# Decoder layer with expert routing on one core: row numbers inside the residual rows, normalised rows scattered as fp16 halves and turned by the loading DMA, two PSUM banks for z

## The chip, the cores and the metric

One core of one Trainium2 chip runs the whole program in one launch. The metric is the time of one execution on the device in microseconds, the median of several runs.

## The reference

The input is x, 4 batches of 512 rows of 512 floats. Three sub-layers follow one another, each with a layer norm (eps 1e-5) in front and a residual sum behind:

```python
x = x + attn(layernorm(x))     # 16 heads of 32, elu features, no softmax
x = x + experts(layernorm(x))  # one of 4 experts for each token, by token id
x = x + ffn(layernorm(x))      # ternary weights, 512 -> 2048 -> 512
# attn:    q = k = elu(x Wqk + bqk), v = silu(x Wv + bv), u = silu(x Wu + bu)
#          out = q (k^T v) within each head; (u * layernorm(out)) Wo + bo
# experts: e = min(clip(id) // 6250, 3); y = (silu(x W[e]^T) * (x W[e]^T)) W[e]^T
# ffn:     (silu(x up^T) * (x gate^T)) down^T, each weight rounded to -1, 0, 1 times its mean magnitude
```

All three weights of the expert layer are the same tensor `ctx`, 4 x 512 x 512. A product there is one matrix z, used as silu(z) * z.

## The kernel before, in words

Rows are handled in 16 tiles of 128 rows (`NT` = 16, four of a batch, `T` = 4; `K` = 4 chunks of 128 columns). Products are made of fp16 halves (a high part and the rest) in three passes of a 128x512 product for each chunk, so one full product is 12 matmuls. `resid` holds all 2048 rows of the residual in SBUF, fp32. Five engines run programs of their own, in fixed order, and meet at semaphores. SP issues all plain loads and the turning ones, in one order and on one queue. POOL issues the indirect scatters and computes the 1/sqrt of each layer norm (`rsqrt`, L307).

**Attention.** The loop over batches runs on every engine (`batch` on POOL L333, ACT L478, DVE L825, PE L1156), pipelined: in batch b the products q, v, k, u of b are mixed with the output projection (`project`, L1121) and the second layer norm of b - 1 (`second_norm`, L802), and with the weights of the later stages (`ctx_part`, `magnitudes`). At its end PE forms k^T v and q (k^T v); ACT copies the four results from PSUM (`o_copies`, L538), sums the magnitudes of a 1 MB piece of weights (`magnitudes`, L471), and starts the next batch with the exponentials of q (L483). DVE takes statistics of the copies (`head_stats`), and before the next batch waits until the scatters of b - 1 have landed, since `n2` is used again.

**Sorting by expert.** The rows are sorted by expert through DRAM. `routing_positions` gives each row its place `pos`. `scatter` (L320) sends a tile of normalised rows, fp32, out of `n2` to `sorted_tokens`. `scatter_residual` (L325) sends a tile of residual rows to `sorted_residual`, and `scatter_ids` (L329) one 4-byte row number of each row to `sorted_ids`. The scatters of batches 0 and 1 are issued in the batches behind them. For batch 2 the normalised rows go early in batch 3 and the residual rows after the last head normalisation. At the end of batch 3 POOL handles one tile after the other: `rsqrt_tile` of tile t, then `scatter` of tile t - 1 (L399 to L406); then a memset that DVE waits for before it makes the next signs, the four residual scatters, and all 16 scatters of row numbers. DVE's part of this is `last_sum` (residual sum, statistics) and `last_norm` (L921 to L962).

**Experts.** `STEPS` = 19 steps; each takes 128 sorted rows (one tile) with one expert, and a tile that has rows of several experts is done several times (`own` masks). SP loads sorted tile i into one of three slots of `n2` (`sorted_tile`, L232); PE transposes it into the bank `tx_ps` (`xs_transpose`, L1306), ACT copies the high half to `x3T` (`xs_hi`, L585) and DVE subtracts for the low half (`xs_lo`, L965). In step i (`expert_step`, L1329) PE does: z of step i (`first`), the transposes of tile i + 1, the second product of step i - 1 (`second`), in steps 0 to 9 the turning of one unit of ternary weights for the last layer (`unit_transposes`, L1265), and the transposes of h. DVE adds the result to the sorted residual (`y_add`, L970), which SP loads a batch at a time (`sorted_residual`, L235). SP's order here (L242 to L267):

```python
sp.wait_ge(s["scattered"], 16 * NT)
for i in range(3): sorted_tile(i)
unit(1, 0)                       # after sign_b >= 1
sp.wait_ge(s["x1_sent"], 16 * NT)
sorted_residual(0)
unit(1, 1); unit(1, 2)           # after sign_b >= 2, 3
for n in range(6):
    sp.wait_ge(s["tx_mm"], n + 1)
    sorted_tile(n + 3)
    if n % 2 == 0: sorted_residual(1 + n // 2)
    unit(2 + n // 3, n % 3)      # after sign_b >= n + 4
```

A unit is 1 MB of weights. `signs_of` (L904) on DVE makes two signed bf16 planes of it. PE fills its wait for the last rows with 100 small matmuls (`keep_busy`, L1303).

**Last layer.** The third layer norm writes halves to `x3h`, and SP turns them with `dma_start_transpose` from SBUF into `x3T` (`x3_turned`, L269). The outputs are scattered to their rows with `row_id`, which SP loads from `sorted_ids`.

Of the kernel before, what the change touches and what calls it, by code (L numbers as in the profile page):

```python
# [31 lines left out]
P = 128  # L32
# [17 lines left out]
def decoder(nc, x, itok, ctx_w, Wqk, bqk, Wv, bv, Wu, bu, Wo, bo, ln_g, ln_b, W_up, W_gate, W_down, out):  # L50
# [5 lines left out]
    def sem(name):  # L56
# [16 lines left out]
    xs_v = xs_dram.rearrange("(c p) d -> p c d", p=P)  # L73
    x1_v = x1_dram.rearrange("(c p) d -> p c d", p=P)
    id_v = id_dram.rearrange("(c p) o -> p (c o)", p=P)


    resid = sb("resid", [P, NT, D])
# [32 lines left out]
    tok_id = sb("tok_id", [P, NT], I32)  # L111
    row_id = sb("row_id", [P, NT], I32)
# [8 lines left out]

    xT = late[:, 0].bitcast(F16).rearrange("p (i k s) -> p i k s", i=2, k=K)
# [18 lines left out]
    xs_slot = [n2[:, i] for i in range(3)]  # L141
# [11 lines left out]
    z_ps, y_ps, tx_ps, th_ps, q_ps = ps[0], ps[1], ps[2], ps[3], ps[4:8]  # L153
# [4 lines left out]
        att_in3 stage_in0 stage_in1 scattered x1_sent id_sent id_in x1_in0 x1_in1 x1_in2 x1_in3 xs_in0 xs_in1 xs_in2 unit_in0 unit_in1 unit_in2  # L158
# [6 lines left out]
        x2_stat x2_aggr x2_norm tk_mm k_copy u_mm u_act kv_mm kv_evac o_mm o_copy o_stat o_aggr o_norm  # L165
        tx_mm xs_hi xs_lo z_mm z_act h_mul th_mm h_hi h_lo y_mm y_evac sign_a sign_b unit_mm unit_copy
# [17 lines left out]
    def _(sp):  # L184
# [47 lines left out]
        def sorted_tile(i):  # L232
            sp.dma_start(xs_slot[i % 3], xs_v[:, i]).then_inc(s[f"xs_in{i % 3}"], 16)

        def sorted_residual(b):  # L235
            sp.dma_start(resid[:, T * b:T * b + T], x1_v[:, T * b:T * b + T]).then_inc(s[f"x1_in{b}"], 16)
# [18 lines left out]
        for n in range(6):  # L255
            sp.wait_ge(s["tx_mm"], n + 1)
            sorted_tile(n + 3)
            if n % 2 == 0:
                sorted_residual(1 + n // 2)
            sp.wait_ge(s["sign_b"], n + 4)  # L260
            unit(2 + n // 3, n % 3)
        for i in range(9, NT):
            sp.wait_ge(s["tx_mm"], i - 2)
            sorted_tile(i)

        sp.wait_ge(s["id_sent"], 16 * NT)
        sp.dma_start(row_id[:, :], id_v, allow_slow_non_contiguous=True).then_inc(s["id_in"], 16)  # L267
# [8 lines left out]
        for b in range(B):  # L276
            x3_turned(b)


    @block.gpsimd  # L280
    def _(pool):
# [10 lines left out]
        def late_constants():  # L292
# [12 lines left out]
            pool.iota(tok_id[:, :], pattern=[[P, NT]], base=0, channel_multiplier=1).then_inc(s["starts_made"], 1)  # L305
# [23 lines left out]
        def scatter_ids(b):  # L329
            for n in range(T * b, T * b + T):  # L330
                pool.indirect_dma_start(id_dram, row_of(n), tok_id[:, n:n + 1], None).then_inc(s["id_sent"], 16)

        def batch(b):  # L333
# [75 lines left out]
        for b in range(B):  # L409
            scatter_ids(b)  # L410
# [4 lines left out]
        def send_out(b):  # L415
            for t in range(T):
                pool.wait_ge(s["out_made"], T * b + t + 1)
                pool.indirect_dma_start(out_rows, bass.IndirectOffsetOnAxis(ap=row_id[:, T * b + t:T * b + t + 1], axis=0),  # L418
# [4 lines left out]
        pool.wait_ge(s["id_in"], 16)  # L423
# [7 lines left out]
        for t in range(T):  # L431
            pool.wait_ge(s[f"out_done{t}"], 16 * B)
# [3 lines left out]
    def _(act):  # L436
# [25 lines left out]
        def gated_hi(b, k):  # L462

            act.wait_ge(s["a_mul"], K * b + k + 1)
# [13 lines left out]
        def batch(b, first, last):  # L478
# [50 lines left out]
            if first:  # L529
                magnitudes(b, 1)  # L530
            o_copies(b)
# [28 lines left out]
        with act.Fori(1, B - 1) as b:  # L560
# [5 lines left out]
        o_copies(B - 1)  # L566
        magnitudes(B - 1, 1)
# [6 lines left out]
        gated_hi(B - 1, 0)  # L574
# [5 lines left out]
        gated_hi(B - 1, 3)  # L580
        unit_copies(0, 0)
        unit_copies(0, 1)


        def xs_hi(i):  # L585
            act.wait_ge(s["tx_mm"], i + 1)
            act.activation(x3T[:, i // T, 0, :, (i % T) * P:(i % T + 1) * P], tx_ps.rearrange("p (k s) -> p k s", k=K),
                           ACT.Copy).then_inc(s["xs_hi"], 1)
# [7 lines left out]
        def expert_step(i):  # L596
            act.wait_ge(s["z_mm"], i + 1)
            act.wait_ge(s["h_mul"], i)
            act.activation(sil, z_ps[:, :], ACT.Silu, scale=1.0 / CTX_SCALE).then_inc(s["z_act"], 1)
            if i + 1 < NT:  # L600
                xs_hi(i + 1)
# [10 lines left out]
        xs_hi(0)  # L612
# [33 lines left out]
    def _(dve):  # L646
# [155 lines left out]
        def second_norm(b, t):  # L802
            normalise(2, n2[:, t], x_tile(T * b + t), t, "x2_norm")
# [21 lines left out]
        def batch(b, first, last):  # L825
# [60 lines left out]
            if first:  # L886
                routing_positions()
            if last:
# [12 lines left out]
            if not first:  # L901
                dve.wait_ge(s["scattered"], 16 * T * b)
# [537 lines left out]
```

## Time and profile before

| | us |
|---|---|
| median of 3 runs | 774.2 |
| lowest and highest | 771.91, 776.83 |
| the profiled execution | 772.51 |
| its span | 770.8 |

The span is the time from the first to the last instruction of the profiled execution; its own time is 1.7 us more. Busy over the span: PE 93%, PE's weight loads (PEld, beside PE) 49%, DVE 49%, ACT 35%, POOL 19%. The mean granted clock of PE is 0.979 of full speed. In the rows, `L1082` is a line of kernel.py, which for products and transposes is the line of a helper; x12 is a count; what stands in brackets is the idle time of the engine ahead of the instruction and what ended it.

### The profile page before, as it was taken

The page shows a single profiled execution, that of the slowest core. Times are in us where ns is not written, and L with a number is a line of the kernel's source. Part 1 is how long each engine was busy: PE and PEld are TensorE (multiplying, and loading weights), DVE is VectorE, ACT ScalarE, POOL GpSimd, SP SyncE. Part 2 cuts the span into 40 slices and gives each one's busy share as a digit, 9 for nine tenths or more (in the row PEclk, how much of TensorE's full clock was granted, in tenths as well). Part 3 has the DMA queues.
Part 4 walks back from the last instruction along what each step waited for, and adds up shares of the span by engine and source line. Part 5 has one row for each costly group of instructions (what it writes and reads, how often), then busy time and mean ns, then how long its engine had stood idle before and what let it go on. Part 6 is the DMA issues. An engine that isn't in the chain of part 4 may idle for free.

```text
span 770.8 us, 11599 instructions
## 1 busy us (share of the span) xinstructions
PE 713.1 (93%) x3979; PEld 379.5 (49%) x4008; DVE 378.3 (49%) x622; ACT 273.2 (35%) x426; POOL 146.5 (19%) x202
## 2 busy tenths in 40 slices
PE   7999999999998852999999999999999999999994
PEld 5465466466464721656554444444444444444441
DVE  5566776776767522566455333353333433342232
ACT  4366455455463420444323222222222223222220
POOL 4204532332344860000000000020000200020001
PEclk9999999999999985999999999999999999999998
DMA  8823045044055579761102000011001200010001
GB/s 244 330 102 118 1 135 193 0 147 181 1 182 200 206 102 179 261 225 42 29 1 49 8 14 14 14 44 38 14 14 14 68 14 14 14 54 1 0 1 54
DMA packets 48182, 64.00 MB, mean 83 GB/s; under 512 B 25360, under 2 KB 25360, under 8 KB 47120
## 3 DMA queue, kind: packets, MB, share of 16 engines
q1 hardware_dynamic: 43792, 50.89, 23.2%
q0 software_dynamic: 4352, 12.60, 4.2%
q8 instruction: 25, 0.41, 0.3%
q14 instruction: 13, 0.11, 0.0%
HBM read 46.69 MB, written 12.59 MB: 77 GB/s over the span
## 4 chain that ended last, share of the span: by engine, by line
PE 76%; DVE 7%; DMA 7%; issue 3%; ACT 3%; SPq 2%; POOL 1%; DVEq 0%; ACTq 0%; POOLq 0%
PE bank L1352 28%; PE bank L1082 25%; PE bank L1362 13%; PE bank L1075 4%; DMA n<-sorted_tokens 3%; DVE region L773 2%; PE bank L1239 2%; PE bank L1275 2%; PE bank L1253 2%; DMA stage<-in_L_ffn_W_up_dram 2%; DVE late L769 1%; SPq L229 1%; DMA w_att<-nrm 1%; DMA stage<-in_L_attn_Wv_dram 1%; PE bank L1413 1%
## 5 line engine op out<-in xcount | busy, mean ns | idle before, releaser
L1352 PE MATMUL bank<-w_att,region 128*128 128x512 f16 (+1 forms) x1024 | 231.2, 379 | 2.6 <-DMA w_att<-nrm 2.6
L1352 PEld LDWEIGHTS bank<-w_att,region 128*128 (+1 forms) x1024 | 100.1, 98 | 123.7 <-issue 3.3
L1045 DVE SCALAR_TENSOR_TENSOR tmp<-tmp,hk,bank 128x512 f32<-128x512 f32 x64 | 47.8, 747 | 155.9 <-PE bank L1352 155.4
L1362 PE MATMUL bank<-region,tmpA 128*128 (+1 forms) x452 | 111.3, 379 | 1.5
L310 POOL TENSOR_SCALAR ve<-mv 128x1 f32<-128x1 f32 (+1 forms) x37 | 9.2, 248 | 452.9 <-DVE mv L983 338.4
L1082 PE MATMUL bank<-late,w_att 128*128 128x512 f16 x384 | 86.5, 381 | 1.9 <-DVE region L816 1.9
L621 ACT ACTIVATE tmp<-bank,qs 128x512 f32<-128x512 f32 x64 | 44.0, 687 | 116.6 <-PE bank L1352 116.6
L628 ACT ACTIVATE tmpA<-tmp 128x512 f16<-128x512 f32 x62 | 39.0, 629 | 120.2 <-DVE tmp L1045 120.2
L1362 PEld LDWEIGHTS bank<-region,tmpA 128*128 128x128 f16 x480 | 46.8, 98 | 56.8 <-DVE stage L1029 0.9
L1049 DVE TENSOR_TENSOR tmpA<-tmp,tmpA 128x512 f16<-128x512 f32 x62 | 42.9, 693 | 44.1 <-ACT tmpA L628 44.1
L1082 PEld LDWEIGHTS bank<-late,w_att 128*128 128x128 f16 x384 | 37.4, 98 | 44.5 <-DVE region L816 2.8
L1082 PE MATMUL bank<-w_moe,w_att 128*128 x228 | 52.4, 380 | 4.6 <-issue 2.9
L1082 PE MATMUL bank<-w_moe,tmpA 128*128 x228 | 53.7, 386 | 0.0
L1082 PE MATMUL bank<-w_att,region 128*128 128x512 f16 x192 | 42.4, 379 | 4.0 <-DVE region L777 2.0
L1082 PE MATMUL bank<-w_att,late 128*128 128x512 f16 x192 | 42.8, 379 | 0.0
L552 ACT ACTIVATE region<-bank 128x512 bf16<-128x512 f32 x48 | 24.8, 605 | 40.6 <-PE bank L1275 40.6
L418 POOL DMA_INDIRECT out_dram<-stage,row_id x16 | 16.2, 1011 | 108.7 <-DVE stage L1029 106.9
L1082 PEld LDWEIGHTS bank<-w_moe,w_att 128*128 x228 | 22.2, 97 | 29.1 <-issue 7.5
L1082 PEld LDWEIGHTS bank<-w_moe,tmpA 128*128 128x128 f16 x228 | 22.6, 100 | 24.9 <-issue 2.3
L977 DVE SCALAR_TENSOR_TENSOR resid<-bank,own,resid 128x512 f32 x19 | 14.3, 750 | 37.6 <-PE bank L1082 23.6
L1075 PE MATMUL bank<-ident,n 128*128 128x128 f32 x64 | 10.1, 283 | 23.3 <-DMA n<-sorted_tokens 23.3
L1082 PEld LDWEIGHTS bank<-w_att,region 128*128 128x128 f16 x192 | 18.3, 98 | 26.9 <-issue 2.7
(145 smaller groups left out, 847.5 us busy)
## 6 DMA issues: line engine op xcount, KB each, us to landing
stage<-in_L_ffn_W_up_dram SPq DMA_DIRECT2D x8, 1024.0 KB, 5.9
stage<-in_L_ffn_W_gate_dram SPq DMA_DIRECT2D x8, 1024.0 KB, 5.4
stage<-in_ctx_dram SPq DMA_DIRECT2D x4, 1024.0 KB, 6.6
stage<-in_L_ffn_W_down_dram SPq DMA_DIRECT2D x4, 1024.0 KB, 7.3
nrm<-in_L_ffn_W_down_dram SPq DMA_DIRECT2D x4, 1024.0 KB, 7.5
n<-sorted_tokens SPq DMA_DIRECT2D x16, 256.0 KB, 5.4
resid<-sorted_residual SPq DMA_DIRECT2D x4, 1024.0 KB, 15.4
resid<-in_x_dram SPq DMA_DIRECT2D x1, 3072.0 KB, 19.1
```

Of the source, the lines that this page charges most:

```text
L418: pool.indirect_dma_start(out_rows, bass.IndirectOffsetOnAxis(ap=row_id[:, T * b + t:T * b + t + 1], axis=0), out_slot[t], None).then_inc( ...
L552: act.activation(dst, src, ACT.Copy).then_inc(s["unit_copy"], 1)
L621: act.activation(sil, up_ps[:, :], ACT.Silu, scale=qs[:, 0:1]).then_inc(s["up_act"], 1)
L628: act.activation(dst[:, cc % 2, 0], h32, ACT.Copy).then_inc(s["hid_hi"], 1)
L773: dve.tensor_tensor(aT[:, 1, k], a32[:, k % 2], aT[:, 0, k], ALU.subtract).then_inc(s["a_lo"], 1)
L1045: dve.scalar_tensor_tensor(out=h32, in0=sil, scalar=hk[:, 0:1], in1=gate_ps[:, :], op0=ALU.mult, op1=ALU.mult).then_inc(s["hid_mul"], 1)
L1049: dve.tensor_tensor(dst[:, cc % 2, 1], h32, dst[:, cc % 2, 0], ALU.subtract).then_inc(s["hid_lo"], 1)
L1075: mm = pe.transpose(dst[:, i * P:(i + 1) * P], src(i), ident[:, :])
L1082: mm = pe.matmul(dst, lhs(*step), rhs(*step), start=(start and n == 0), stop=(stop and n == len(steps) - 1))
L1239: mm = pe.matmul(kv_ps[:, cut], kk[:, t, cut], vv[:, t, cut], start=(t == 0), stop=(t == T - 1))
L1352: mm = pe.matmul(dst, w[:, bass.ds(cf_c, 1), k * P:(k + 1) * P].rearrange("p a n -> p (a n)"), x3T[:, bass.ds(b, 1), i, k].rearrange("p a ...
L1362: mm = pe.matmul(ffy_ps[t][:, :], hid[:, parity, i, t * P:(t + 1) * P], tern[2][:, bass.ds(c, 1)].rearrange("p a n -> p (a n)"), start=(st ...
```

## The change

- `resid` becomes the first 512 words of rows of 513 (`rows`). The 513th holds the row number, made by the iota that filled `tok_id`. `sorted_residual` has rows of 513 words (2052 bytes), scatters and loads move them whole, and `row_id` is a view of the 513th words. `scatter_ids`, `sorted_ids`, and the load of `row_id` are gone.
- The second layer norm writes fp32 rows to `region[:, 5]` (the place of aT), for the last batch to `region[:, 1]`. ACT copies them to fp16 high halves (`n2_hi`), DVE subtracts for the low halves (`n2_lo`), both in `n2h`, which is `n2` seen as fp16. `scatter` waits for `n2_lo` and sends 2 x 512 halves of each row, as many bytes as before.
- In the experts' stage `sorted_tile` is a `dma_start_transpose` from DRAM straight to its place in `x3T`. `xs_transpose`, `xs_hi` and `xs_lo` are gone; SP goes by `z_mm` in place of `tx_mm`, PE's `first` waits for the tile's own transfer.
- z has two PSUM banks (the old one and the one of the tile transposes).
- Orders: POOL's `rs_o` comes ahead of the scatters in each batch; those of batch 2 move behind the last head normalisation's rsqrt. ACT's batches 1 and 2 are written out instead of looped. `n2_hi` stands ahead of `o_copies` in batches 1 and 2, `n2_lo` ahead of `head_stats`. DVE's wait for landed scatters at a batch's end goes. SP instead of POOL waits for the last output scatters.

```diff
-    xs_dram = nc.dram_tensor("sorted_tokens", (NT * P, D), F32, kind="Internal").ap()
-    x1_dram = nc.dram_tensor("sorted_residual", (NT * P, D), F32, kind="Internal").ap()
-    id_dram = nc.dram_tensor("sorted_ids", (NT * P, 1), I32, kind="Internal").ap()
+    xs_dram = nc.dram_tensor("sorted_halves", (NT * P, 2 * D), F16, kind="Internal").ap()
+    x1_dram = nc.dram_tensor("sorted_residual", (NT * P, D + 1), F32, kind="Internal").ap()
-    resid = sb("resid", [P, NT, D])
+    rows = sb("rows", [P, NT, D + 1])
+    resid = rows[:, :, 0:D]
+    row_id = rows[:, :, :].bitcast(I32)[:, :, D:D + 1]
+    n2h = n2[:].rearrange("p t d -> p (t d)").bitcast(F16).rearrange("p (t h d) -> p t h d", t=T, h=2)
+    second_rows = lambda b: region[:, 1] if isinstance(b, int) and b == B - 1 else region[:, 5]
...
         def sorted_tile(i):
-            sp.dma_start(xs_slot[i % 3], xs_v[:, i]).then_inc(s[f"xs_in{i % 3}"], 16)
+            sp.dma_start_transpose(
+                out=x3T[:, i // T, :, :, (i % T) * P:(i % T + 1) * P].rearrange("p i k s -> p (i k) s"),
+                in_=xs_v[i]).then_inc(s[f"xs_in{i % 4}"], 16)
...
         def scatter(b, t):
-            pool.wait_ge(s["x2_norm"], T * b + t + 1)
-            pool.indirect_dma_start(xs_dram, row_of(T * b + t), n2[:, t], None).then_inc(s["scattered"], 16)
+            pool.wait_ge(s["n2_lo"], T * b + t + 1)
+            pool.indirect_dma_start(xs_dram, row_of(T * b + t), n2h[:, t].rearrange("p h d -> p (h d)"), None).then_inc(s["scattered"], 16)
         def scatter_residual(b):
             for n in range(T * b, T * b + T):
-                pool.indirect_dma_start(x1_dram, row_of(n), resid[:, n], None).then_inc(s["x1_sent"], 16)
+                pool.indirect_dma_start(x1_dram, row_of(n), rows[:, n], None).then_inc(s["x1_sent"], 16)
...
-            if b > 0:
+            if b < B - 1:
+                rsqrt(1, "o_aggr", T * b + T, slice(0, T), "rs_o", b)
+            if 0 < b < B - 1:
                 for t in range(T):
                     scatter(b - 1, t)
-            if b < B - 1:
-                rsqrt(1, "o_aggr", T * b + T, slice(0, T), "rs_o", b)
...
         for t in range(T):
             rsqrt_tile(1, "o_aggr", T * (B - 1), t, "rs_o_last")
+        for t in range(T):
+            scatter(B - 2, t)
         scatter_residual(B - 2)
...
-        for b in range(B):
-            scatter_ids(b)
...
+            else:
+                for t in range(T):
+                    n2_hi(b - 1, t)
             o_copies(b)
             magnitudes(b, 2)
...
+        def n2_hi(b, t):
+            act.wait_ge(s["x2_norm"], T * b + t + 1)
+            if t == 0 and b > 0:
+                act.wait_ge(s["scattered"], 16 * T * b)
+            act.activation(n2h[:, t, 0], second_rows(b)[:, t], ACT.Copy).then_inc(s["n2_hi"], 1)
...
         o_copies(B - 1)
+        for t in range(T):
+            n2_hi(B - 2, t)
         magnitudes(B - 1, 1)
...
+        def n2_lo(b, t):
+            dve.wait_ge(s["n2_hi"], T * b + t + 1)
+            dve.tensor_tensor(n2h[:, t, 1], second_rows(b)[:, t], n2h[:, t, 0], ALU.subtract).then_inc(s["n2_lo"], 1)
...
         last_norm(0)
         last_sum(2)
         last_norm(1)
+        n2_lo(B - 1, 0)
         last_sum(3)
         last_norm(2)
+        n2_lo(B - 1, 1)
         last_norm(3)
+        n2_lo(B - 1, 2)
+        n2_lo(B - 1, 3)
         dve.wait_ge(s["scatter_out"], 1)
         signs_of(0, 1)
...
         def first(i):
             w = weights_of(i)
             off = pe.value_load(step_off[0:1, i:i + 1], min_val=0, max_val=(B - 1) * 2 * K * S + S - P)
-            pe.wait_ge(s["xs_lo"], min(i, NT - 1) + 1)
-            pe.wait_ge(s["h_mul"], i)
-            product(z_ps[:, :], lambda i, j, k: sorted_T[:, bass.ds(off + (i * K + k) * S, P)], w).then_inc(s["z_mm"], 1)
+            if i < NT:
+                pe.wait_ge(s[f"xs_in{i % 4}"], 16 * (i // 4 + 1))
+            if i > 1:
+                pe.wait_ge(s["h_mul"], i - 1)
+            product(z_ps[i % 2][:, :], lambda i, j, k: sorted_T[:, bass.ds(off + (i * K + k) * S, P)], w).then_inc(s["z_mm"], 1)
```

## Rows read from the trace of the kernel before

**Rows 1.** Busy time by stretch: start:end, length, engines, PEclk, DMA share, GB/s

```profile
283.00:304.00 21.00, 0.15 (x1) 0.15 (x2) 4.43 (x5) 0.00 (x0) 2.45 (x3) 0.52 1.00 163
304.00:425.00 121.00, 116.77 (x772) 67.45 (x772) 66.40 (x93) 44.23 (x82) 3.15 (x8) 0.98 0.35 109
```

**Rows 2.** Chain that ended last, 255 to 304 us: start, us, what

```profile
255.65 2.71 DMA sorted_tokens<-n,pos
...
259.71 12.90 DMA stage<-in_L_ffn_W_up_dram
...
275.13 7.74 SPq L229
...
282.91 20.90 DMA n<-sorted_tokens
```

**Rows 3.** Busy time by finer stretches, columns as in rows 1

```profile
272.00:280.00 8.00, 7.59 (x63) 4.57 (x61) 3.68 (x4) 3.57 (x7) 6.22 (x6) 1.00 0.77 31
280.00:290.00 10.00, 0.50 (x3) 0.01 (x1) 0.00 (x0) 0.60 (x1) 4.79 (x5) 0.69 1.01 177
...
304.00:312.00 8.00, 7.84 (x56) 4.73 (x57) 1.44 (x2) 3.15 (x6) 0.00 (x0) 0.77 0.97 347
```

**Rows 4.** Timeline of POOL: first and last of the 16 scatters of row numbers

```profile
263.46 2.29 POOL L331 DMA_INDIRECT sorted_ids<-tok_id,pos  x1 [0.30 <-issue]
...
285.10 0.95 POOL L331 DMA_INDIRECT sorted_ids<-tok_id,pos  x1 [0.30 <-issue]
```

**Rows 5.** DMA issues of these two, us to landing at the end

```profile
sorted_ids<-tok_id,pos POOLq DMA_INDIRECT x1, 6.7
...
sorted_ids<-tok_id,pos POOLq DMA_INDIRECT x1, 18.1
```

**Rows 6.** Chain that ended last, step 3 of the experts

```profile
311.33 2.76 PE bank L1082 x12
314.09 0.44 PE bank L1075 x4
314.53 2.59 PE bank L1082 x12
317.12 1.79 PE bank L1275 x32
...
319.53 2.76 PE bank L1082 x12
```

**Rows 7.** Timeline of the tail of batch 3, to the first expert product

```profile
249.52 1.08 POOL L323 DMA_INDIRECT sorted_tokens<-n,pos  x1 [0.18 <-issue]
...
252.45 5.75 PE L1089 MATMUL bank<-ones 128*128 128x128 bf16 x100
...
253.84 0.55 DVE L656 TENSOR_SCALAR n<-resid,mv,rs 128x512 f32<-128x512 f32 x1 [0.77 <-POOL rs L312]
...
256.76 1.29 DVE L911 TENSOR_SCALAR late<-stage,thr 128x2048 bf16<-128x2048 f32 x1 [2.38 <-POOL halfs L407]
...
263.41 2.76 PE L1082 MATMUL bank<-w_moe,w_att 128*128 x12 [1.71 <-DVE w_att L968]
```

**Rows 8.** Instructions that touch nrm: durations ns min/median/max, first and last start

```profile
L992 DVE TENSOR_TENSOR nrm<-nrm x16: 680/683/686, 403.1 to 670.9; 128x512 f16<-128x512 f32 x16
L272 SPq DMA_TRANSPOSE w_att<-nrm x16: 1232/1233/1345, 403.9 to 671.6; - x16
```

**Rows 9.** DMA issues of the page, median us to landing at the end

```profile
w_att<-nrm SPq DMA_TRANSPOSE x16, 3.0
```

**Rows 10.** Timeline at the boundary of batches 2 and 3

```profile
178.99 0.60 ACT L542 ACTIVATE region<-bank 128x512 f32<-128x512 f32 x1 [0.30 <-PE bank L1253]
...
182.79 0.69 ACT L483 ACTIVATE tmp<-bank,cols 128x512 f32<-128x512 f32 x1
...
184.85 0.39 PE L1082 MATMUL bank<-late,w_att 128*128 128x512 f16 x1 [0.28 <-DVE region L816]
```

**Rows 11.** Timeline of DVE: signs of the unit loaded in the hole

```profile
299.50 1.29 DVE L911 TENSOR_SCALAR late<-stage,thr 128x2048 bf16<-128x2048 f32 x1 [7.84 <-DMA stage<-in_L_ffn_W_gate_dram]
```

More of the change, by code:

```diff
@@ L152, in decoder @@
     acc, tr, kv_ps, o_ps, prep = ps[0:2], ps[2:4], ps[4], ps[5:7], ps[7]
-    z_ps, y_ps, tx_ps, th_ps, q_ps = ps[0], ps[1], ps[2], ps[3], ps[4:8]
+    z_ps, y_ps, th_ps, q_ps = (ps[0], ps[2]), ps[1], ps[3], ps[4:8]
     ffy_ps, up_ps, gate_ps = ps[0:4], ps[4], ps[5]
     names = """x_first0 x_first1 x_first2 x_first3 x_rest cols_in rows_in tok_in att_in0 att_in1 att_in2
-        att_in3 stage_in0 stage_in1 scattered x1_sent id_sent id_in x1_in0 x1_in1 x1_in2 x1_in3 xs_in0 xs_in1 xs_in2 unit_in0 unit_in1 unit_in2
+        att_in3 stage_in0 stage_in1 scattered x1_sent x1_in0 x1_in1 x1_in2 x1_in3 xs_in0 xs_in1 xs_in2 xs_in3 unit_in0 unit_in1 unit_in2
         out_done0 out_done1 out_done2 out_done3
@@ L430, in _ @@
         send_out(B - 1)
-        for t in range(T):
-            pool.wait_ge(s[f"out_done{t}"], 16 * B)
     @block.scalar
@@ L460, in affine, with gated_hi @@
                            scale=cols[:, 2, k:k + 1]).then_inc(s["n_aff"], 1)
-        def gated_hi(b, k):
+        def gated_hi(b, k, sent=None):
+            if sent is not None:
+                act.wait_ge(s["n2_lo"], sent)
             act.wait_ge(s["a_mul"], K * b + k + 1)
@@ L559, in _ @@
         batch(0, True, False)
-        with act.Fori(1, B - 1) as b:
+        for b in range(1, B - 1):
             batch(b, False, False)
@@ L566, in _ @@
         o_copies(B - 1)
+        for t in range(T):
+            n2_hi(B - 2, t)
         magnitudes(B - 1, 1)
@@ L580, in _ @@
         gated_hi(B - 1, 3)
+        for t in range(T):
+            n2_hi(B - 1, t)
         unit_copies(0, 0)
         unit_copies(0, 1)
[L585 to L588, printed above, removed]
         def x3_hi(i):
@@ L598, in expert_step @@
             act.wait_ge(s["h_mul"], i)
-            act.activation(sil, z_ps[:, :], ACT.Silu, scale=1.0 / CTX_SCALE).then_inc(s["z_act"], 1)
-            if i + 1 < NT:
-                xs_hi(i + 1)
+            act.activation(sil, z_ps[i % 2][:, :], ACT.Silu, scale=1.0 / CTX_SCALE).then_inc(s["z_act"], 1)
             if i == 0:
@@ L802, in second_norm @@
         def second_norm(b, t):
-            normalise(2, n2[:, t], x_tile(T * b + t), t, "x2_norm")
+            normalise(2, second_rows(b)[:, t], x_tile(T * b + t), t, "x2_norm")
+        def n2_lo(b, t):
+            dve.wait_ge(s["n2_hi"], T * b + t + 1)
+            dve.tensor_tensor(n2h[:, t, 1], second_rows(b)[:, t], n2h[:, t, 0], ALU.subtract).then_inc(s["n2_lo"], 1)
         def ctx_lo(b, k):
@@ L887, in batch @@
                 routing_positions()
+            elif not last:
+                for t in range(T):
+                    n2_lo(b - 1, t)
             if last:
@@ L900, in batch @@
                     aggregate(1, t, "o_stat", T * b + T, "o_aggr")
-            if not first:
-                dve.wait_ge(s["scattered"], 16 * T * b)
+            if last:
+                for t in range(T):
+                    n2_lo(b - 1, t)
         def signs_of(g, j):
@@ L952, in _ @@
         signs_of(0, 0)
+        dve.wait_ge(s["n2_lo"], T * (B - 1))
         last_sum(0)
@@ L957, in _ @@
         last_norm(1)
+        n2_lo(B - 1, 0)
         last_sum(3)
         last_norm(2)
+        n2_lo(B - 1, 1)
         last_norm(3)
+        n2_lo(B - 1, 2)
+        n2_lo(B - 1, 3)
         dve.wait_ge(s["scatter_out"], 1)
         signs_of(0, 1)
-        def xs_lo(i):
-            dve.wait_ge(s["xs_hi"], i + 1)
-            hi, lo = (x3T[:, i // T, h, :, (i % T) * P:(i % T + 1) * P] for h in range(2))
-            dve.tensor_tensor(lo, tx_ps.rearrange("p (k s) -> p k s", k=K), hi, ALU.subtract).then_inc(s["xs_lo"], 1)
         def y_add(i):
@@ L1303, in _ @@
         unit_transposes(0, 1)
-        def xs_transpose(i):
-            pe.wait_ge(s[f"xs_in{i % 3}"], 16 * (i // 3 + 1))
-            pe.wait_ge(s["xs_lo"], i)
-            transposes(tx_ps, lambda k: xs_slot[i % 3][:, k * P:(k + 1) * P]).then_inc(s["tx_mm"], 1)
         def weights_of(i):
```

38 lines of the change are left out of this document (11 added, 27 removed).

## The prediction

> **What bounds the kernel now.** I read first the busy times by stretch. From 304 to 425 us, the stage of the experts, PE is busy 116.8 of 121 us at the full clock, so PE is the bound there. From 283 to 304 it is busy 0.15 of 21 us, its clock is down to 0.52, and the DMA engines' share is 1.00 at only 163 GB/s [rows 1]. This is the one large hole of the program, and every part of the change that touches a transfer has to be read against it. The chain of waits crosses it with four pieces: the last scatter of normalised rows lands 2.71 us after its issue at 255.65; a 1 MB weight load takes 12.90 us; SP sits 7.74 us on the issue of the next one; and a 256 KB load of sorted rows, the fourth tile, takes 20.90 us and releases PE at 303.8 [rows 2].
>
> Why is the queue so slow? The finer stretches tell: from 272 to 280 the engines are busy 0.77 and move 31 GB/s, from 280 to 290 they move 177, and from 304 to 312, with the same kinds of loads, 347 [rows 3]. What runs in the slow stretch and not in the fast one are the 16 scatters of row numbers, 128 writes of 4 bytes each, issued by POOL from 263.46 to 285.10 [rows 4]. The first lands after 6.7 us, the last after 18.1, that is at 303.2 [rows 4, 5]. So 15 of them land in 303.2 - 270.2 = 33 us: 2.2 us for one, 17 ns for a write, and the loads are slow for exactly as long. I take the row numbers as the cause of the hole. That is an inference from coincidence in time, and the rivals price the case in which it is false.
>
> **The change part by part.**
>
> (1) Row numbers as a 513th word of the residual row. The 16 scatters of POOL go with their 20 us of issue, and with them, by the reading above, the clog. What bounds PE then? In the frame of the old trace, let PE's first expert product end at E. Until the fourth tile is needed PE has: tile transposes out, so weights' turning 1.79 + transposes of h 0.44 + about 0.2 of issue = 2.4, then two full steps of 2.6 + 2.6 + 1.79 + 0.44 + 0.2 = 7.65 [rows 6]. So it asks for tile 3 at E + 17.8. In the old trace that product began at 263.41 [rows 7], thus E = 266.2, and the fourth began at 311.33 [rows 6], which is 45.2 after E. Gain 27.4, if the queue delivers. Does it? From the first tile on it has to move the load of step 1, the first residual MB, two more MB of weights and tile 3 with its share of scatters: about 5 MB, 14.4 us at the 347 GB/s of [rows 3], beginning some 3.5 us before E. It is done near E + 11 to E + 14 (at 250 GB/s E + 17), ahead of the demand, with little to spare. At the other end, nothing of the clog goes (see the rival). I take the full 27.4.
>
> (2) Loading DMA turns the tiles. PE loses 4 transposes a tile, 0.44 us in the chain, ACT a copy and DVE a subtraction. PE is the bound of these steps, so tiles 4 to 15 give 12 x 0.44 = 5.3 us [rows 6] (those of the first four are in the 17.8 above). ACT and DVE had room there, their share is worth nothing. The price is 16 turning loads. The only such transfers in the trace, from SBUF, take 1.23 us to issue and 3.0 to land on a quiet queue [rows 8, 9], and each has about three steps, 22 us, before PE wants it: nothing, except for tile 0, which is on the path. There 3.0 stands for the 2.7 of the plain load, but a copy and a subtraction (1.3) go: between -1 and +3 from a DRAM source never seen here, taken as 0 with the shift in (4).
>
> (3) Halves made on the chip: one DVE subtraction (0.68 [rows 8]) and one ACT copy (0.60, as the copy of o in [rows 10]) per tile, before the scatter. In batches 1 and 2 four copies, 2.4 us, stand in front of ACT's four copies of o, and those release PE's last products and are followed on ACT by a magnitude sum, a table load and the exponential at 182.79, on which, by way of DVE, PE waits until 184.85 [rows 10]. ACT is idle for a part of this now (0.30 us before the copy of o shown), which takes some of the 2.4. I get the exponential 1.2 later and PE's next free bank 1.6 later. Between 0 and 2.4 for each of two boundaries: +3.2. In the last batch POOL no longer scatters ahead of the last head normalisation, but ACT has four more copies ahead of its last u activations: +1.0 (-1 to +2.5). The DVE's wait on landed scatters goes; they had long landed, nothing.
>
> (4) The tail of the last batch. Now each normalised tile goes to POOL at once: normalised 253.84, its scatter issued 255.65, DVE's next signs at 256.76, first product at 263.41 [rows 2, 7]. In the new order DVE does norm(1) before halves(0), norm(2) before halves(1), norm(3) before halves(2), while POOL does rsqrt(t + 1) only after scatter(t - 1), which waits for these halves. Now POOL makes three rounds between 249.52 and 255.65, 2.05 us each, of which the scatter is 1.08 and the rsqrt with its gaps the other 0.97. The new round is rsqrt 0.97, DVE's normalise 0.55 and subtraction 0.68, the scatter 1.08 and some 0.3 of hand-overs: 3.6 us. By following it through, with DVE's sums between, I have scatter 0 at +3.1 and scatters 2 and 3 at +5 to +6 against the old issue times (1.0 of it from part 3). DVE's signs, which wait behind the last scatter, go from 256.8 to 262.5, the turning of that unit ends at 266.8, tile 0 lands at 267.3, and the first product begins near 267.4 instead of 263.4: +4.0, of which +1.0 is counted. PE, whose filler now ends at 258.2 [rows 7], is then idle from 259.2 to 265.0. In the old hole the clock was still full for 0.38 x 10 us after 280 and came back 3.7 us after PE resumed at 304 [rows 3]; so it will just fall to its lower level here (1.2 of 2.4 GHz) and make the next 3.7 us do half their work: +1.6 (0 to 2). Sum +4.6 (+2 to +8).
>
> (5) POOL's order (rs_o before the scatters) frees nothing that is waited for; behind it the bias additions of POOL start when its ten issues are done, just in time. ACT's batches written out instead of looped, the last waits on SP instead of POOL, and one bank more for z: PE already had to wait for h before its transposes, so nothing; -2 to +1 together.
>
> Sum: -27.4 - 5.3 + 3.2 + 1.0 + 4.6 = -23.9. The profiled execution took 772.5 us (span 770.8 and 1.7 around it): 748.6. The median shown is 1.7 higher, 774.2, which would give 750.3. I take 750. The forecast's own range is 743 to 757.
>
> The Trainium skill ("DMA: Bandwidth & Descriptors", section on how a descriptor splits into AXI transactions) has a rule that speaks against part 1: a run is cut into pieces of 256 bytes and one leftover, and a start off a 256-byte boundary costs a further piece. A row of 2052 bytes then carries a leftover of 4 bytes. No row here shows such a transfer; by the rule the row numbers' small writes would still be there, which is the mechanism of the first rival below.
>
> **The rivals.**
> *The small write rides along.* Residual rows of 2052 bytes start and end off any boundary, so each has one or two small writes of its own. At 17 ns each, 2.2 to 4.4 us for a scatter of 128 rows, where issue takes 1.3. The four of the last batch land some 4 x (3.3 - 1.3) = 8 us later, the four before them push the last tiles by up to 2, and the queue behind them, tile 3 last, comes 10 us after the above: 27.4 becomes 17 to 18, time 759. For: the same count of small writes. Against: row numbers of one tile fall on a few neighbouring lines of an 8 KB tensor, these edges are spread over 4 MB.
> *The clog isn't the row numbers'* but that of bulk loads that read freshly scattered rows. Then the queue is as slow as before. PE still gains something, as it no longer stands before tile 3 in step 2 but only for the unit of weights (in at 299.5 [rows 11], signs until 302, their turning) and then the product: fourth product near 308 instead of 311.3. With 5.3 that is -8.6, and the shifts of 3 and 4 only move what waits anyway: 764 (762 to 768). For: the last slow stretch has 8 KB runs with it. Against: 347 GB/s with the same loads as soon as the last row number is in.
> *The turning load becomes the bound* (the slower side). From first landing to the last tile the queue has 16 turned tiles and 10 MB (29 us at 347 GB/s). The old program had about 131 us from the first tile until the last had to be there, so break-even is at (131 - 29)/16 = 6.4 us of queue per turned tile. At 8 us, say because 256-byte pieces out of DRAM are slow or because turning keeps other loads from running, the stage ends 16 x 1.6 = 26 us later than break-even: 798. For: it is unseen from DRAM. Against: 3.0 us from issue to landing from SBUF, with 1.23 of it issue.
> *More than the sum:* the tail of part 4 hides better, and the boundaries cost nothing: 743.
>
> **How the numbers follow.** Forecast 0.55 (750), small write 0.15 (759), clog stays 0.13 (764), turning loads 0.07 (798), more than the sum 0.10 (743). Range 742 to 768: below it 0.07 or so, above it the turning loads and the edge of the third case. The measurement can tell about 1%, that is 766.5 and 781.9: faster 0.83, within 1% 0.11, slower 0.06.
>
> **What would show it.** Right: no stretch with DMA share 1.00 below 200 GB/s after the scatters; PE's hole before the fourth tile gone or under 3 us; step period 7.7 instead of 8.2 and 5.6 instead of 6.05; first expert product 7 us later than before in the program's time; each of the batch boundaries 1 and 2 longer by 1 to 2 us; a short fall of the clock just ahead of the first step. Wrong: residual scatters landing long after issue (first rival), a hole of 20 us that stays with no row numbers in flight (second), PE waiting for a turned tile in steps past the fourth (third).

## The result, and the profile after

The changed kernel takes 747.3 us (743.9 to 749.9, 4 runs), the kernel before on the same chip 775.1 (771.91 to 776.83, 4 runs): ratio 0.964 [0.959, 0.970]. The forecast was 750, range 742 to 768. The profiled executions went from 772.51 to 746.75, -25.8, where the sum said -23.9; the spans from 770.8 to 744.9.

The hole is gone. Busy time by stretch of the changed kernel (columns as in rows 1):

```profile
255.00:266.00 11.00, 6.09 (x110) 5.92 (x107) 5.42 (x9) 3.21 (x6) 7.33 (x10) 1.00 0.25 95
266.00:272.00 6.00, 3.38 (x33) 3.20 (x33) 3.26 (x3) 2.32 (x4) 4.99 (x4) 0.72 0.69 154
272.00:280.00 8.00, 7.34 (x60) 4.55 (x60) 2.25 (x3) 3.05 (x6) 0.00 (x0) 1.00 0.86 254
280.00:290.00 10.00, 9.78 (x72) 5.60 (x71) 5.24 (x7) 3.75 (x7) 0.00 (x0) 1.00 1.10 323
```

Where [rows 3] had 31 and 177 GB/s from 272 to 290, these have 254 and 323, and PE is busy 9.78 of 10 us from 280 to 290. What is left of idle PE in these stretches is mostly ahead of the experts: 5.8 us and then 1.7, with the clock at 0.72 of full speed from 266 to 272. The timeline of PE there, which answers to [rows 7] and to the hole of [rows 1, 2]:

```profile
255.35 5.75 PE L1094 MATMUL bank<-ones 128*128 128x128 bf16 x100
266.92 3.27 PE L1280 MATMUL bank<-ident_b,late 128*128 128x128 bf16 x32 [5.83 <-DVE late L920]
271.90 2.76 PE L1087 MATMUL bank<-w_moe,w_att 128*128 x12 [1.70 <-DMA w_att<-sorted_halves]
274.49 1.95 PE L1280 MATMUL bank<-ident_b,late 128*128 128x128 bf16 x32
...
277.55 2.76 PE L1087 MATMUL bank<-w_moe,w_att 128*128 x12 [0.66 <-issue]
...
293.55 2.76 PE L1087 MATMUL bank<-w_moe,w_att 128*128 x12 [0.19 <-issue]
```

The first expert product starts at 271.90 (before 263.41), the fourth at 293.55 (before 311.33). Cutting both programs at the same instructions tells where the 25.9 us of span went:

| stretch | before | after | difference | by the sum |
|---|---|---|---|---|
| start to first expert product | 263.41 | 271.90 | +8.5 | +7.2 |
| first to fourth product | 47.92 | 21.65 | -26.3 | -25.8 (-27.4, and the clock's +1.6) |
| fourth to the last layer's first product | 113.99 | 109.83 | -4.2 | -5.3 |
| from there to POOL's last scatter | 336.96 | 336.28 | -0.7 | 0 |
| last scatter to the end of the span | 8.52 | 5.24 | -3.3 | 0 (-2 to +1) |

The tail of batch 3 on POOL (compare the 249.52 of [rows 7] and the 255.65 of [rows 2]):

```profile
254.53 1.08 POOL L323 DMA_INDIRECT sorted_halves<-n,pos  x1 [2.27 <-DVE n L807]
...
258.01 1.09 POOL L323 DMA_INDIRECT sorted_halves<-n,pos  x1 [1.47 <-DVE n L807]
...
261.51 1.46 POOL L323 DMA_INDIRECT sorted_halves<-n,pos  x1 [1.47 <-DVE n L807]
263.27 0.96 POOL L323 DMA_INDIRECT sorted_halves<-n,pos  x1 [0.30 <-issue]
```

A round is 3.5 us, POOL waiting in each 1.47 for the subtraction that makes the halves; the last scatter is 7.6 later than before. The boundary of batches 2 and 3 (compare [rows 10]):

```profile
177.21 2.19 ACT L546 ACTIVATE n<-region 128x512 f16<-128x512 f32 x4
179.29 1.08 ACT L540 ACTIVATE region<-bank 128x512 f32<-128x512 f32 x2
...
185.82 0.69 ACT L478 ACTIVATE tmp<-bank,cols 128x512 f32<-128x512 f32 x1
```

The four copies stand ahead of the copies of o, as the diff has it, and the exponential goes from 182.79 to 185.82. PE's product of q goes from 184.85 to 187.88 (+3.0), 1.9 of it already there at the boundary before (127.56 to 129.47). So one boundary costs 1.9 and the other 1.1.

The transfers, from the DMA issues of the page and of two single moments (KB each, us to landing at the end; over several issues the median):

```profile
rows<-sorted_residual SPq DMA_DIRECT2D x4, 1026.0 KB, 8.8
...
w_att<-sorted_halves SPq DMA_TRANSPOSE x1, 5.7
...
sorted_residual<-rows,pos POOLq DMA_INDIRECT x1, 7.6
```

The first line is of the page; the other two are tile 0's turning load, issued at 266.00, and the last residual scatter, issued at 270.95. Tile 0 lands after 5.7 us, where [rows 9] had 3.0; PE waits 1.70 for it. No product of a later step waits for a turned tile.

### The profile page after: what moved, and what is told of

It is laid out like the page before. It is cut to its first block, busy times and chain, and to the rows that moved or that the text cites. A ratio compares the mean times of both kernels' runs of the same rounds, so it can differ in the third digit from the quotient of the medians.

```text
span 744.9 us, 11387 instructions
## 1 busy us (share of the span) xinstructions
PE 707.7 (95%) x3915; PEld 373.7 (50%) x3944; DVE 376.6 (51%) x622; ACT 273.5 (37%) x426; POOL 124.9 (17%) x186
## 4 chain that ended last, share of the span: by engine, by line
PE 75%; DVE 7%; ACT 5%; DMA 4%; issue 4%; POOL 2%; SPq 1%; DVEq 0%; POOLq 0%; ACTq 0%
PE bank L1351 30%; PE bank L1087 23%; PE bank L1361 14%; PE bank L1080 3%; DVE region L773 2%; PE bank L1280 2%; PE bank L1244 2%; PE bank L1258 1%; DMA stage<-in_L_ffn_W_gate_dram 1%; DVE late L769 1%; ACT stage L470 1%; DMA w_att<-nrm 1%; DMA sorted_residual<-rows,pos 1%; DMA stage<-in_L_attn_Wv_dram 1%; POOL sorted_residual L327 1%
## 5 line engine op out<-in xcount | busy, mean ns | idle before, releaser
L414 POOL DMA_INDIRECT out_dram<-stage,rows x16 | 16.2, 1012 | 107.7 <-DVE stage L1034 105.9
L1087 PEld LDWEIGHTS bank<-w_att,region 128*128 128x128 f16 x192 | 18.3, 98 | 25.9 <-DVE region L773 2.2
L1280 PE MATMUL bank<-ident_b,late 128*128 128x128 bf16 x384 | 24.7, 225 | 6.1 <-DVE late L920 6.1
L1087 PEld LDWEIGHTS bank<-w_att,late 128*128 128x128 f16 x192 | 18.7, 98 | 21.3 <-DVE region L777 0.5
```

Of the source, the lines that this page charges most:

```text
L1087: mm = pe.matmul(dst, lhs(*step), rhs(*step), start=(start and n == 0), stop=(stop and n == len(steps) - 1))
L1280: mm = pe.matmul(q_ps[r][:, cut], signs[:, u % 2, h, r, cut], ident_b[:, :], start=(h == 0), stop=(h == 1))
```

## The experiments

Each run has the kernel before beside it on the same chip: 772.8 (9 runs) for e1 to e4, 774.4 (7 runs) for e5 to e8, 773.8 (9 runs) for e9 and e10. "On before" and "on after" say which kernel the edit is made on.

### e1, e2: the row numbers moved, and put back

e1 is on before: the same 16 scatters, issued after the experts.

```diff
-        for b in range(B):
-            scatter_ids(b)
...
         for t in range(T):
             third_rsqrt(t)
+        for b in range(B):
+            scatter_ids(b)
```

SP's load of `row_id`, with its wait for the scatters, goes behind `x3_turned(0)`.

> The kernel before, with its 16 scatters of row numbers issued only after the experts' stage (POOL, behind the first four rsqrt of the third layer norm) and the load of row_id behind the first four turned tiles of the last layer. Nothing else is changed. If the row numbers' small writes clog the queue: the hole of 23 us before the fourth tile shrinks to under 6 us, the first residual load lands within 6 us instead of 17.6, and the time falls by 17 to 23 us, to about 0.973 of before. If the clog comes of bulk loads that read freshly scattered rows: the hole stays above 15 us and the time within 5 us of before. The small writes should then land in about 33 us during the last layer, beside no load, and cost nothing there.

e2 is on after: a tensor for row numbers, 16 scatters of them behind the last residual scatter, and a wait for them at the end of SP.

```diff
         scatter_residual(B - 1)
+        for n in range(NT):
+            pool.indirect_dma_start(id_dram, row_of(n), tok_id[:, n:n + 1], None).then_inc(s["id_sent"], 16)
```

> The changed kernel plus the 16 scatters of 4-byte row numbers, in the place they had before, to a tensor of their own that nobody reads (SP waits for them at the very end). If the row numbers make the hole: PE idles 12 to 20 us before the third or fourth step of the experts and the time is 12 to 20 us above the changed kernel's, 762 us or so. If it was the old kernel's plain loads of sorted rows, or their place in the queue: within 3 us of the changed kernel.

e1: 764.6 us, ratio 0.990 [0.987, 0.992]. e2: 765.6, 0.990 [0.988, 0.993]; the changed kernel has 0.964, so e2 is 18.3 us above it in the medians and about 20 by the ratios. A stretch of e1, then two of e2 (columns as in rows 1):

```profile
272.00:280.00 8.00, 7.84 (x65) 4.99 (x64) 4.66 (x7) 3.64 (x7) 0.00 (x0) 1.00 1.02 399
```

```profile
280.00:290.00 10.00, 6.48 (x46) 3.60 (x45) 3.53 (x4) 1.57 (x3) 7.87 (x8) 0.96 0.72 109
290.00:298.00 8.00, 5.01 (x28) 3.00 (x26) 0.42 (x1) 2.55 (x5) 2.32 (x3) 0.84 1.17 128
```

With the row numbers gone from here and nothing else changed, the old program's loads run at 399 GB/s where they had 31, and its fourth product starts at 290.26, 21.1 earlier. With the row numbers put back, the new program falls to 109 and 128 GB/s. That shows the cause of the hole from both sides.

But e1 gains 8 us, where 17 to 23 were expected. Of the 21.1 us at the fourth product, 10.3 are lost again by the first product of the last layer (414.52 - 290.26 = 124.3 us, against 114.0 before) and 2.3 behind it. The chain that ended last, at the start of its last layer, tells why (start, us, what):

```profile
394.59 0.69 DVE nrm L991
395.30 7.94 DMA w_att<-nrm
...
405.07 0.69 DVE nrm L991
405.78 8.60 DMA w_att<-nrm
414.38 0.14 issue
414.52 3.57 PE bank L1351 x8
```

The turning of the last layer's tiles, 3.0 us in [rows 9], takes 7.94 and 8.60 beside the row numbers, and PE waits for it. I had taken this as a place where they cost nothing. They slow these small turning loads as they slowed the bulk loads.

### e5, e9: the same small writes, farther apart

Both on before, at the old place and time: 128 writes of 4 bytes each, 16 times. Only the address of a row number is multiplied, by 512 words (2048 bytes apart) or by 16 (64 bytes).

```diff
-    id_dram = nc.dram_tensor("sorted_ids", (NT * P, 1), I32, kind="Internal").ap()
+    id_dram = nc.dram_tensor("sorted_ids", (NT * P * 512, 1), I32, kind="Internal").ap()
...
-                pool.indirect_dma_start(id_dram, row_of(n), tok_id[:, n:n + 1], None).then_inc(s["id_sent"], 16)
+                pool.indirect_dma_start(id_dram, bass.IndirectOffsetOnAxis(ap=far[:, n:n + 1], axis=0), tok_id[:, n:n + 1], None).then_inc(s["id_sent"], 16)
...
+            route(dve.tensor_scalar(far[:, :], pos_f[:, :], float(512), None, ALU.mult))
```

> The kernel before, with each row number written 2048 bytes apart (index 512 times the place) instead of 4 bytes apart; as many writes, of the same 4 bytes, in the same order and at the same time. If it is neighbouring writes on a few lines that clog the queue: the scatters of row numbers land within 4 us of their issue, the hole before the fourth tile falls under 6 us, and the time goes to about 750 (the last layer is not disturbed either). If it is the small write as such: the hole stays at 15 to 23 us and the time at 765 to 775.

> The kernel before, with each row number written 64 bytes apart (index 16 times the place). Beside the run at 2048 bytes apart, which had no clog. If only writes into the same 64 bytes hinder each other: no clog, 752 us. If neighbours within a larger line (256 or 512 bytes, or the whole few KB) hinder each other: a hole remains, of a size between 5 and 23 us, 757 to 774 us.

e5: 752.15 (one run), e9: 758.3 (one run). POOL issues them as before (e5: 264.2 to 286.8). A stretch of e5, then the same of e9:

```profile
272.00:280.00 8.00, 7.79 (x65) 4.96 (x63) 4.41 (x6) 3.64 (x7) 6.47 (x6) 1.00 0.98 373
```

```profile
272.00:280.00 8.00, 3.56 (x15) 1.57 (x14) 2.50 (x3) 1.79 (x3) 6.36 (x6) 0.82 1.04 405
```

373 and 405 GB/s with the row numbers in flight, where neighbouring addresses gave 31. The row numbers' own landings, as far as the traces pair them, take 3.8 us in both, where [rows 5] has 6.7 and 18.1. Each time there are as many writes, of the same 4 bytes, so neither their number nor their size is enough to clog the queue: they also have to be neighbours, and 64 bytes from one to the next clear it. Why neighbours hinder each other no run shows, nor what distances between 4 and 64 bytes do. e5 has nothing of the change in it but the clear queue, and already gains 22.2 us of the 27.8 that the changed kernel gains in the medians. Between its first product and its fourth PE waits for a transfer once, 2.30 us, and the fourth starts at 290.59:

```profile
283.21 1.07 PE L1077 MATMUL bank<-ident,n 128*128 128x128 f32 x4 [2.30 <-DMA n<-sorted_tokens]
...
290.59 2.76 PE L1084 MATMUL bank<-w_moe,w_att 128*128 x12 [0.20 <-issue]
```

e9 takes 6.1 us more than e5, which is a time that the expectation had given to a hole that remains (757 to 774). Its queue doesn't have one; what it has is idle time of PE under "issue", not under a transfer:

```profile
278.34 5.30 PE L1084 MATMUL bank<-w_moe,tmpA 128*128 x12 [4.44 <-issue]
...
286.90 0.28 PE L1277 MATMUL bank<-ident_b,late 128*128 128x128 bf16 x2 [0.50 <-issue]
...
288.49 2.76 PE L1084 MATMUL bank<-w_moe,w_att 128*128 x12 [0.86 <-issue]
```

The last line is the third product, which starts 10.3 us later than in e5 (288.49 against 278.15). Of that, 0.8 stand already at the first product; idle time under "issue" adds 6.1, and the product at the lower clock, 5.30 instead of 2.75, another 2.5. Then 4.2 come back, since e9 doesn't wait for the fourth tile: its fourth product starts at 296.70, 6.1 behind e5's. DVE idles in the same piece, 7.8 us under "issue" up to 277.5. What held them stays open, and one run can't tell whether it belongs to the spacing.

### e3: residual rows without the word

On after: rows of 512 words in DRAM, so that the row number isn't sent or read back. The scatters of the result then have no row numbers to go by, and the order of the output's rows isn't the reference's.

```diff
-    x1_dram = nc.dram_tensor("sorted_residual", (NT * P, D + 1), F32, kind="Internal").ap()
+    x1_dram = nc.dram_tensor("sorted_residual", (NT * P, D), F32, kind="Internal").ap()
...
-                pool.indirect_dma_start(x1_dram, row_of(n), rows[:, n], None).then_inc(s["x1_sent"], 16)
+                pool.indirect_dma_start(x1_dram, row_of(n), rows[:, n, 0:D], None).then_inc(s["x1_sent"], 16)
```

> The changed kernel with residual rows of 512 words in DRAM: scatter and load leave out the 513th word, so the row numbers are not sorted and output rows go to other places than the reference's. Prices the small write that rides along. If the edges of 2052-byte rows cost as the row numbers did (17 ns each): the last residual scatter, issued 270.95, lands 4 us or more earlier after its issue than the 7.6 us it took, and the time falls by 1 to 3 us. If they cost nothing: landing within 1 us of 7.6, time the same within 1 us.

746.25 us, 0.964 [0.961, 0.967]: no difference. But the transfer does change. The last residual scatter, which took 7.6 in the changed kernel, and the median of all 16, of e3 and then of the changed kernel:

```profile
sorted_residual<-rows,pos POOLq DMA_INDIRECT x1, 4.8
...
sorted_residual<-rows,pos POOLq DMA_INDIRECT x16, 3.8
```

```profile
sorted_residual<-rows,pos POOLq DMA_INDIRECT x16, 5.2
```

So rows of 2052 bytes land later than rows of 2048, and nobody waits for it. How much later depends on what else is in the queue. In the four scatters from 184 to 200 us it is 1.0 (3.7 against 2.7). Of the last four, the last has 2.8, but the first lands sooner with the longer rows (7.0 against 7.5). The 2.2 to 4.4 us for each scatter that the first rival gave are not what the scatters show outside the traffic at the end. The Trainium skill ("DMA: Bandwidth & Descriptors", section "How a descriptor splits into AXI transactions") counts the leftover of each row as a transaction of its own; the later landings agree with it in sign, and it gives no price to compare. By its count a row of 2052 bytes makes nine transactions wherever it starts, so the further piece that the prediction adds for a start off a boundary doesn't come here.

### e4: the last waits on POOL

On after, the one item of part 5 that sits at the end of the program.

```diff
-        for t in range(T):
-            sp.wait_ge(s[f"out_done{t}"], 16 * B)
...
         send_out(B - 1)
+        for t in range(T):
+            pool.wait_ge(s[f"out_done{t}"], 16 * B)
```

> The changed kernel with the four last waits (output scatters landed) back on POOL. From POOL's last scatter to the end of the span the old program took 8.5 us and the changed one 5.2. If the place of these waits is the cause: 3.3 us more than the changed kernel, between last scatter and end. If it is the offsets' place or anything else of the output: no difference.

749.1 us, 0.969 [0.966, 0.971]. The last scatter of the result, of this kernel and then of after:

```profile
741.41 0.96 POOL L412 DMA_INDIRECT out_dram<-stage,rows  x1 [0.77 <-DVE stage L1034]
```

```profile
739.66 0.96 POOL L414 DMA_INDIRECT out_dram<-stage,rows  x1 [0.77 <-DVE stage L1034]
```

From there to the end of the span: 748.6 - 741.4 = 7.2 us with the waits on POOL, 744.9 - 739.7 = 5.2 on SP, 8.5 in the kernel before. So the place of the wait is worth 2.0 of the 3.3 us. The other 1.3 stand in every kernel that scatters row numbers by themselves: e2, which sends them again and has its waits on SP, takes 763.5 - 757.0 = 6.5 us from its last scatter to the end, while e3, e6, e7, e8 and e10 all have 5.2, and e1, e5 and e9 all have the 8.5. What it is about the row numbers that the end of the program waits for, no run shows.

### e6, e7, e8: the two prices taken out

e6 takes the wait of [1.47 <-DVE] out of POOL's rounds: rsqrt 0 to 2 first, then the scatters, and DVE makes halves(t) ahead of norm(t + 1).

```diff
-        rsqrt_tile(2, "x2_aggr", T * (B - 1), 0, "rs2_last")
+        for t in range(3):
+            rsqrt_tile(2, "x2_aggr", T * (B - 1), t, "rs2_last")
+        scatter(B - 1, 0)
+        rsqrt_tile(2, "x2_aggr", T * (B - 1), 3, "rs2_last")
         for t in range(1, T):
-            rsqrt_tile(2, "x2_aggr", T * (B - 1), t, "rs2_last")
-            scatter(B - 1, t - 1)
-        scatter(B - 1, T - 1)
+            scatter(B - 1, t)
...
         last_sum(2)
+        n2_lo(B - 1, 0)
         last_norm(1)
-        n2_lo(B - 1, 0)
         last_sum(3)
+        n2_lo(B - 1, 1)
         last_norm(2)
-        n2_lo(B - 1, 1)
```

> The changed kernel with another order at the tail of batch 3: POOL does the rsqrt of tiles 0, 1 and 2 ahead of the first scatter, and DVE makes the halves of tiles 0 and 1 ahead of the normalisation of tiles 1 and 2. If the tail was a chain of rsqrt behind a scatter behind halves, as forecast: the last scatter of halves is issued 3 to 4 us earlier than at 263.3 and the time falls by 2 to 4 us, the clock's dip included. If the landing of the residual scatters or of tile 0 sets the start of the experts: less than 1 us.

e7 moves the four copies of batches 1 and 2 between first_norm (0, 1) and (2, 3), and two of the subtractions ahead of kv_mask.

```diff
-            first_norm(b + 1)
+            first_norm(b + 1, (0, 1))
+            if not first:
+                for t in range(T):
+                    n2_hi(b - 1, t)
+            first_norm(b + 1, (2, 3))
             if first:
                 magnitudes(b, 1)
-            else:
-                for t in range(T):
-                    n2_hi(b - 1, t)
...
+            if not first and not last:
+                n2_lo(b - 1, 0)
+                n2_lo(b - 1, 1)
```

e8 has both edits.

> The changed kernel with the high halves of batches 1 and 2 copied between ACT's two pairs of copies of the first norm, where ACT idles 3.2 us, and two of the four low halves made on DVE ahead of the kv mask. If the batch boundary costs what it does (1.9 and 1.1 us) through ACT's four copies in front of the copies of o: both are gained back, time -2.5 to -3. If the cost sits on DVE's four subtractions instead: less than half of it.

> Both edits of the two runs before together, on the changed kernel. If they are independent, the sum of their gains: 5 to 7 us under the changed kernel, 741 or so. If the start of the experts is set by something else, about 3.

e6: 744.8, 0.963 [0.960, 0.966]. e7: 741.3, 0.960 [0.956, 0.964]. e8, both together: 741.9, 0.959 [0.956, 0.961]. Against the changed kernel's 0.964 these intervals overlap or just touch, so the traces have to speak. In e7 the products of q restart at 126.86 and 183.80 instead of 129.47 and 187.88: the boundary's price is gone, and 1.1 more. In e6 the last scatter of halves comes 2.4 us earlier (260.88 against 263.27), in e8 by 2.2 against e7 (257.00 against 259.17), but less arrives at PE. The timeline of PE of e8:

```profile
260.65 3.43 PE L1285 MATMUL bank<-ident_b,late 128*128 128x128 bf16 x32 [3.05 <-DVE late L925]
266.19 4.37 PE L1092 MATMUL bank<-w_moe,w_att 128*128 x12 [2.11 <-DMA w_att<-sorted_halves]
...
273.44 2.76 PE L1092 MATMUL bank<-w_moe,w_att 128*128 x12 [0.57 <-issue]
```

The first product starts 1.9 us ahead of e7's 268.11 but takes 4.37 instead of 2.76, and the turning behind it runs partly slow: by the second product (273.44 against 273.76) 0.3 of the 1.9 us is left. That the first product is slow here need not be the doing of the edit. e3 is the changed kernel up to this point except for the width of the residual rows, and there the same product takes 4.29 where the changed kernel's profiled execution has 2.76:

```profile
272.09 4.29 PE L1087 MATMUL bank<-w_moe,w_att 128*128 x12 [1.90 <-DMA w_att<-sorted_halves]
```

e2 has 4.37 in the same place. In each of these PE has idled 5.83 us and then about 1.9 for tile 0, as in the changed kernel; the granted clock from 266 to 272 was 0.50 in e2 and e3 and 0.72 in the changed kernel. So the profiled executions differ in when the clock is back, and the 1.6 us can't be charged to e8. What the runs say is that e8 (741.9) is no faster than e7 (741.3): a gain of the second edit isn't shown.

### e10: more filler, so that the clock stays up

On e8: 150 filler products instead of 100 ahead of that turning, and 30 behind it.

> The kernel of the last run (both edits) with more small filler matmuls on PE at the end of batch 3: 150 in place of 100 ahead of the turning of unit (0, 1), which fill the 3.05 us it idles there, and 30 behind it, for the 2.1 us until tile 0 lands. If the clock's dip costs at the start of the experts: the first product takes 2.76 us instead of 4.37, the turning 1.95 instead of 3.43 (that one hidden), and the time falls by 1.5 to 2.5 us, to 740. If the start is set by transfers alone: no change.

743.1 us (5 runs), 0.959 [0.956, 0.961]: the same as e8.

```profile
265.35 2.76 PE L1092 MATMUL bank<-w_moe,w_att 128*128 x12 [1.41 <-DMA w_att<-sorted_halves]
...
270.98 2.76 PE L1092 MATMUL bank<-w_moe,w_att 128*128 x12 [0.63 <-issue]
...
278.47 3.37 PE L1285 MATMUL bank<-ident_b,late 128*128 128x128 bf16 x32 [2.15 <-DVE late L925]
```

The forecast of 740 fails. The clock is held (2.76 for the first product), the second starts 2.5 us ahead of e8's, and then PE waits 2.15 for the next unit's signs, behind a weight load of 11.2 us in the chain, and the clock falls there. The third product starts at 282.34, in e8 at 281.23. So what PE gains ahead of this load, it waits for behind it. The load itself is issued 0.9 us earlier than in e8 (264.69 against 265.63) and lands 1.9 later (275.9 against 274.0); why, no run shows.

## Why the prediction was right

**Part 1, the row numbers: right, in cause and in size.** They were inferred from coincidence in time; e1 and e2 show it, and the stretches of e5 and e9, one run each, show that it takes neighbouring addresses. The second rival (bulk loads of fresh rows, 764) falls: the same loads run at 399 GB/s in e1. First to fourth product, with tile 0 at hand: the step count gave 17.8 + 2.76 = 20.6 us (its terms add up to 17.7); measured 21.65, and most of the rest stands in two waits, 0.66 where 0.2 was counted and 0.26 where none was. The stretch with DMA share 1.00 below 200 GB/s is gone, as forecast.

**Part 2, turned tiles: right for tiles 4 to 15, mis-sized for tile 0.** The chain of the changed kernel, against the 8.2 of [rows 6]:

```profile
309.11 5.35 PE bank L1087 x24
314.46 1.79 PE bank L1280 x32
316.25 0.44 PE bank L1080 x4
316.69 0.25 issue
316.94 5.35 PE bank L1087 x24
```

Step 7.8 (7.7 forecast), later 5.7 (5.6). Of the 5.3 us 4.2 arrived; 0.5 of the rest is one wait for DVE at 388.3, behind a turning load of the last layer that took 4.79 instead of 3.0, and 0.6 has no row of its own. The term that was off is the landing of tile 0: 3.0 was taken from a quiet queue, and this load runs beside the residual scatters; 5.7 measured, 2.7 more. Against the old path (2.7 of the plain load and 1.3 of copy and subtraction) that is +1.7, where 0 was taken and -1 to +3 given. In e7 and e8 PE waits 1.9 and 2.1 for the same tile. The third rival needed 6.4 us of queue for each turned tile; from 280 to 322 the queue moves 303 to 333 GB/s with these loads among the others, and PE waits for none of them past tile 0, so it falls.

**Part 3, boundaries: right in sum.** 1.9 + 1.1 against 2 x 1.6; in e7 it is gone with the place of the copies. e7 moves two subtractions as well and doesn't part the two; that ACT's exponential already comes 3.0 later behind its copies speaks for the copies. The last batch was off: signs of the first unit pair there come 2.9 us later (245.23 against 242.33), all of it from the two boundaries, so the +1.0 was 0.

**Part 4, the tail: the round right (3.6 forecast, 3.5 measured), three sizes off.** POOL's last scatter came at +7.6, the forecast had +8.2 to +9.2 with the boundaries and the last batch's +1.0 in it. So tile 0's load was issued about 1.4 earlier than forecast, and with its 2.7 more to landing the first product started at +8.5 instead of +7.2. The clock fell, as forecast, but its +1.6 is not in the profiled time: the slow piece is the turning (3.27 instead of 1.95, +1.3), which ended 1.70 before tile 0 was in, so it cost nothing, and the first product ran at full speed. That the forecast fits the profiled execution so well here is in part luck: the missing 1.6 of the clock stands against the 1.3 of tile 0 and the waits of part 1. In e2 and e3 the first product does pay 1.6 and 1.5 (4.37 and 4.29 instead of 2.76), as the forecast had it.

**Part 5: missed.** -3.3 us behind the last scatter, outside the -2 to +1: 2.0 by the place of the waits, which was put at nothing, and 1.3 that go with the row numbers (e4). It is why the sum, -23.9, lies 1.9 short of the -25.8; the other stretches together gave 1.3 less than forecast. In the medians the forecast is 2.7 off (747.3 against 750): these 1.9, and 1.1 because the median now lies 0.6 above the profiled execution and not 1.7, less 0.3 of rounding.

**The first rival** is half true: the longer row costs 1.0 us in landing in quieter traffic and 2.8 in the last scatter, and nothing in time (e3).

## What to carry to other kernels

When a queue is busy and moves little, look at which transfers are in flight only then, and test it from both sides: take them away, and put them back in the faster kernel. Small scattered writes to neighbouring addresses are worth moving into a row that is sent anyway, or, at the price of one multiplication, spreading over memory: e5, one run, got 22 of the 28 us by that alone. A gain ahead of a stretch that waits for transfers can be given back in it (e10), so cut at common instructions and see at which of them a gain is still there. And before a slow product is charged to an edit, look for the same product in other runs whose program is the same up to there: here the clock came back at different times in them (e3, e8).

## What was not expected of the hardware

- With number and size unchanged, spacing decides. 2048 writes of 4 bytes took the queue to 31 GB/s as neighbours and left it at 405 at 64 bytes apart (e9) and 373 at 2048 (e5). The Trainium skill ("DMA: Bandwidth & Descriptors", section "Specifications") has transfers below 512 bytes under line rate, since they are done as a read-modify-write. All three are below it, and the rule makes no difference between them; the measurement does.
- SP's issue of a turning load takes 1.23 us on a quiet queue [rows 8]; in the experts' stage of the changed kernel the longest takes 5.42, in e2 16.33. SP's next load is issued only behind it (at 296.07 in e2, the turning load having begun at 279.70).
- The end of the program is 2.0 us shorter when SP rather than POOL, which issued the scatters, waits for them (e4).
